# DLRM tower with pairwise field interactions on one Trainium2 core: ScalarE makes one-hot units ahead of its drains, and the last batch chunk has two looked-up field groups instead of four

## The reference

```python
e = jnp.stack([tbl_0[ids[:, 0]], ..., tbl_39[ids[:, 39]]], axis=1)      # 2048 x 40 x 32
i, j = np.triu_indices(40, k=1)
z = jnp.einsum('bke,kef,bkf->bk', e[:, i, :], L0_rec_W, e[:, j, :])      # 2048 x 780
h = jnp.concatenate([z, dense_ctx], axis=1)                              # 2048 x 796
h = jnp.maximum(h @ W_top1 + b_top1, 0.0)                                # 512
h = jnp.maximum(h @ W_top2 + b_top2, 0.0)                                # 256
y = h @ W_top3                                                           # 1
```

## Time and profile before

| | us |
|---|---|
| median of 3 runs | 693.56 |
| the profiled execution's own time | 690.86 |
| its span | 689.1 |
| TensorE busy | 653.5 (95%) |
| VectorE busy | 537.8 (78%) |
| POOL busy | 374.5 (54%) |
| ScalarE busy | 277.2 (40%) |
| TensorE's mean granted clock | 0.993 of full |

### The profile page before, as it was taken

One profiled execution on the slowest core, in us unless ns is written; L12 is line 12 of the kernel. 1 busy time (PEld: TensorE's weight loads), 2 busy tenths in 40 slices (PEclk: granted clock), 3 DMA queues, 4 the chain that ended last, 5 costly groups with the idle time before them and its releaser, 6 DMA issues.

```text
span 689.1 us, 11819 instructions
## 1 busy us (share of the span) xinstructions
PE 653.5 (95%) x5120; PEld 203.5 (30%) x5120; DVE 537.8 (78%) x515; ACT 277.2 (40%) x196; POOL 374.5 (54%) x391
## 2 busy tenths in 40 slices
PE   3779889888999999999999999999999999999998
PEld 1222223222233333233333323333332323223233
DVE  6776789889879898879768989797767878789910
ACT  3634855876636455647034545655210000100002
POOL 5774576666566566565556556565564666560000
PEclk9989999999999999999999999999999999999999
DMA  7392111203320303012311202001202201101000
GB/s 250 103 377 86 48 52 41 58 13 87 79 68 11 87 12 88 10 43 58 87 23 46 87 11 57 10 14 46 66 13 55 55 13 20 48 12 48 1 1 0
DMA packets 26707, 39.40 MB, mean 57 GB/s; under 512 B 9168, under 2 KB 15456, under 8 KB 26528
## 3 DMA queue, kind: packets, MB, share of 16 engines
q1 hardware_dynamic: 14336, 32.33, 14.5%
q0 software_dynamic: 12288, 6.32, 6.1%
q10 hardware_dynamic: 32, 0.01, 0.0%
HBM read 22.88 MB, written 0.01 MB: 33 GB/s over the span
## 4 chain that ended last, share of the span: by engine, by line
PE 89%; ACT 5%; DMA 2%; DVE 2%; SPq 1%; issue 1%; DVEq 0%; ACTq 0%
PE tps L680 31%; PE zps L702 27%; PE mlp_ps L753 15%; PE mlp_ps L733 12%; PE tps L753 4%; ACT hot L534 2%; ACT hot L531 2%; DVE prods L660 2%; DMA eT<-eT 1%; DMA ids<-in_hot_ids 1%; SPq L432 1%; PE zps L689 0%; ACT zs L500 0%; ACT eT L540 0%; PE mlp_ps L758 0%
## 5 line engine op out<-in xcount | busy, mean ns | idle before, releaser
L660 DVE TENSOR_TENSOR prods<-tps,eT 128x1024 f32<-128x1024 f32 x400 | 468.6, 1217 | 109.9 <-PE tps L680 106.4
L484 POOL DMA_INDIRECT rows<-in_table,idx x384 | 373.8, 974 | 245.9 <-DVE prods L660 136.9
L680 PE MATMUL tps<-eT,weights 32*128 32x512 f32 x1600 | 242.9, 643 | 8.3 <-ACT eT L540 6.2
L702 PE MATMUL zps<-prods,select 128*32 128x512 f32 x1600 | 207.4, 607 | 0.8 <-DVE prods L660 0.3
L531 ACT ACTIVATE hot<-ids,minus_code 128x2048 bf16<-128x2048 int16 x57 | 113.7, 1994 | 41.1 <-PE mlp_ps L733 41.0
L733 PE MATMUL mlp_ps<-hot,parts 128*32 128x512 bf16 x1536 | 106.0, 390 | 23.6 <-ACT hot L534 10.8
L534 ACT ACTIVATE hot<-hot,ones 128x2048 bf16<-128x2048 bf16 x57 | 114.1, 2002 | 1.9
L680 PEld LDWEIGHTS tps<-eT,weights 32*128 32x128 f32 x1600 | 70.7, 183 | 135.9 <-DVE prods L660 72.1
L753 PE MATMUL mlp_ps<-zs,w1s 128*128 128x512 f32 x182 | 85.6, 608 | 0.0
L702 PEld LDWEIGHTS zps<-prods,select 128*32 128x32 f32 x1600 | 35.5, 108 | 150.7 <-DVE prods L660 88.5
L500 ACT ACTIVATE zs<-zps 128x512 f32<-128x512 f32 x28 | 16.7, 597 | 150.7 <-PE zps L702 144.5
(11 more groups left out here) (28 smaller groups left out, 44.6 us busy)
## 6 DMA issues: line engine op xcount, KB each, us to landing
ids<-in_hot_ids SPq DMA_DIRECT2D x16, 512.0 KB, 4.9
eT<-eT SPq DMA_DIRECT2D x40, 192.0 KB
rows<-in_table,idx POOLq DMA_INDIRECT x384
eT<-eT SPq DMA_DIRECT2D x40, 128.0 KB
eT<-eT SPq DMA_DIRECT2D x40, 64.0 KB
zs<-in_hot_table SPq DMA_DIRECT2D x4, 512.0 KB, 8.5
w1s<-in_w SPq DMA_DIRECT2D x1, 1792.0 KB
weights<-in_wt SPq DMA_DIRECT2D x1, 960.0 KB, 8.9
```

The source lines that it names most:

```text
L484: pool.indirect_dma_start(rows[:, k % ROW_SLOTS, m * EMB:(m + 1) * EMB], None, table, bass.IndirectOffsetOnAxis(ap=idx[:, g, t, m:m + 1], ...
L660: dve.tensor_tensor(prods[:, at % PROD_SLOTS, 2 * half:2 * half + 2, :], tps[:, (2 * at + half) % PAIR_BANKS, :, :], tiles, ALU.mult).then ...
L680: last = pe.matmul(tps[:, (2 * at + half) % PAIR_BANKS, bank, :], weights[part, n, :], eT[part, slot_of(t, g), :], start=True, stop=True)
L702: last = pe.matmul(zps[EMB * r:EMB * (r + 1), :], select[:, off:off + EMB], prods[:, at % PROD_SLOTS, bank, :], start=kt < KT - 1 and slot ...
```

## The change

It does five things. (1) In the last chunk only groups 0 and 1 are hot; groups 2 and 3 are gathered like the others, so 14 groups are looked up and 26 gathered. (2) The MLP steps done during chunk 2 are cut into twos and threes, as those during chunk 3 are, and units follow only behind as many output tiles as there are hot groups. (3) In chunks 0 and 1 (`HOTS[...][0] < 2`) ScalarE's units of a cycle are made ahead of that cycle's drains. (4) Of groups 2 and 3 of chunk 0 ScalarE makes one unit each, number 5, and not numbers 3 and 7; VectorE makes the others, the fourth unit of group 2 already before its `rest(2, 1)`. (5) VectorE's units of chunk 1's groups are made four quads ahead of use and not three.

```diff
@@ -112,7 +112,7 @@
-HOT_COUNT = (4, 4, 4, 4)
+HOT_COUNT = (4, 4, 4, 2)
@@ -130,7 +130,7 @@
     for at, tile in enumerate(tiles.values()):
-        starts = list(range(0, len(tile) - 1, 2)) if t == CHUNKS - 1 else [0, 4] if at < 2 else [0]
+        starts = list(range(0, len(tile) - 1, 2)) if t > 1 else [0, 4] if at < 2 else [0]
@@ -162,7 +162,7 @@
             blocks.append(batch)
-            if hots and batch[-1][2] == 0 and batch[-1][4] == KT - 1:
+            if batch[-1][2] == 0 and batch[-1][3] < len(hots) and batch[-1][4] == KT - 1:
                 blocks += [(hots[batch[-1][3]], u) for u in range(0, UNITS, 2)]
@@ -189,7 +189,7 @@
     t, g = HOTS[h]
-    return [g > 1 and u % 4 == 3, ((h - HOT_COUNT[0]) * UNITS + u) % 3 > 0, u % 2 == 1][min(t, 2)]
+    return [g > 1 and u == 5, ((h - HOT_COUNT[0]) * UNITS + u) % 3 > 0, u % 2 == 1][min(t, 2)]
@@ -203,14 +203,15 @@
 for unit in range(UNITS):
-    MAKES[1 + unit // HOT_SLOTS].append((3, unit))
+    MAKES[3 if by_scalar(3, unit) else 1 + unit // HOT_SLOTS].append((3, unit))
...
-            MAKES[side_at - (2 if by_scalar(*item[1:]) else 3)].append(item[1:])
+            MAKES[side_at - (2 if by_scalar(*item[1:]) else 4)].append(item[1:])
@@ -561,15 +562,19 @@
             act.wait_ge(consts_built, 2 + Q)
-            make_unit(2, 3)
             round_part(3, 0)
-            make_unit(2, 7)
+            make_unit(2, 5)
             round_part(3, 1)
-            make_unit(3, 3)
             for cycle in CYCLES:
                 at = cycle[0]
                 if at == QUADS + 1:
                     act.wait_ge(mlp_loaded, 16 * 5)
+                units = [unit for quad in cycle for unit in MAKES[quad] if by_scalar(*unit) and unit != (2, 5)]
+                for unit in units:
+                    if HOTS[unit[0]][0] < 2:
+                        make_unit(*unit)
                 drain_tiles(steps_of(at))
                 drain_sums(at - 1)
...
-                for unit in [unit for quad in cycle for unit in MAKES[quad]]:
-                    if by_scalar(*unit) and unit not in ((2, 3), (2, 7), (3, 3)):
+                for unit in units:
+                    if HOTS[unit[0]][0] > 1:
                         make_unit(*unit)
@@ -634,7 +639,7 @@
             rest(2, 0)
-            for u in range(HOT_SLOTS - 1):
+            for u in range(HOT_SLOTS):
                 make_unit(2, u)
```

## The result

In the comparison that the forecast was made for, the changed kernel takes 663.36 us (median of 4 runs, 662.41 to 664.96) and the kernel before 693.29 us (4 runs, 691.1 to 695.09): a ratio of 0.957, 95% interval 0.954 to 0.961, 30 us less. The forecast was 666.1, with 660.5 to 677.

What follows compares the result with a forecast made beforehand. TensorE, busy 95%, was taken as the bound, so time is gained where it stands or gets less work. Terms 5.9 + 10.4 + 1.2 + 10.0 = 27.5 off 690.86 give 663.4, plus 2.7 a 666.1 us median; range 660.5 to 677.

Steps and rivals of the forecast that it cites:

- (a): Chunk 0's start, quads 0 to 6: earlier copies of hot groups 2 and 3 save 5.9 us.
- (b): Chunk 0: all five look-up stalls for ScalarE's units go, 10.4 us; eight quads take 21.7 us.
- (c): Chunk 0: the clock dip behind the stall near 76 us goes with it, saving 1.2 us.
- the loop did not tighten towards TensorE's 20.5: Chunk 0's upper bound: eight quads at 20.5 us, not 21.7, would gain 5 x 1.2 us more.
- VectorE did not close up further: Rival in chunk 0: VectorE's backlog takes half the stall gain and all the clock gain; 672.5 us, chance 0.12.
- (d): Chunk 2: 16 units fewer and finer MLP batches save 10.0 us, with VectorE not taking over.
- (e): 32 more gathers, two transposes, two fewer id loads: no cost, covered by POOL's waits and VectorE's open time.
- The rival that ended on the slow side: Chunk 3: gathers come late because POOL can't go faster, delaying the last transpose by 43.7 us; 737 us, chance 0.03.

Runs made afterwards that it cites:

- e1: Changed kernel with four hot groups in the last chunk and the old MLP batches restored, leaving chunk 0's parts; 808.9 us, 0.987 of the kernel before.
- e4: Kernel before with only chunk 1's ScalarE units made ahead of the cycle's drains; 814.1 us, 0.988 of the kernel before.
- e10: Changed kernel with only the first of each group's 16 gathers issued, the rest left zero; 663.4 us, 0.793 of the kernel before.
- e2: Kernel before with only the last chunk's two hot groups (26 gathered) and chunk 2's fine batches added; 852.3 us, 1.039 of the kernel before.
- e12: Changed kernel with each of the 416 indirect gathers replaced by a plain copy of the same shape; 664.2 us, 0.815 of the kernel before.
- e11: Changed kernel with the gathered ids set to zero, so each gather fetches its tables' first rows; 838.4 us, 1.027 of the kernel before.
- e9: Changed kernel run once more without any edit; 857.4 us, 1.025 of the kernel before.
- e6: Changed kernel with chunk 2's MLP steps back in the old coarse batches; 844.3 us, 1.032 of the kernel before.
- e7: Changed kernel with no hot group in the last chunk, so 28 gathered groups; 928.8 us, 1.135 of the kernel before.

## Why the prediction was right, and where it was not

**Against the first comparison it was right** in its sum and in the stretches, though not in every step inside them. These sizes are read from one trace of the whole change. No part was run alone under those conditions, so that each part causes its own share is argued from where the time left, and supported by the waits in e1 to e4.

*(a) Start.* -5.9 was forecast. From the first product to quad 6 it took 64.68 - 32.54 = 32.1 us and now 59.94 - 33.92 = 26.0: -6.1. The mechanism is the forecast one. ScalarE copies group 2 as soon as its sum is there, and the transform waits 0.70 us, not 4.68:

```profile
42.94 0.60 ACT L541 ACTIVATE eT<-mlp_ps 128x512 f32<-128x512 f32 x1 [7.84 <-PE mlp_ps L738]
...
43.59 0.71 PE L685 MATMUL tps<-eT,weights 32*128 32x512 f32 x4 [0.70 <-ACT eT L541]
```

But the steps inside don't match, and that their sum does is in part luck. The transform was to start at 41.0 and started at 43.59, 9.7 us behind the first product and not 8.5. Group 3's copy was to start at 50.5 and started at 53.40; measured from the first product it came 4.4 us earlier than before, not 5.9. The rest was made up behind it. The forecast let quad 6 wait for the mixed tile as before, while now VectorE works from 55.29 to 61.17 without a pause, and quad 6's products wait for no DMA.

*(b) and (c) Stalls and clock.* -10.4 and -1.2 were forecast. Quad 6 to quad 50 took 195.73 - 64.68 = 131.05 and now 179.98 - 59.94 = 120.04: -11.0. The 40 quads from 10 to 50 take 109.0 us and not 117.1, 21.8 for eight against the 21.7 forecast. So the loop did not tighten towards TensorE's 20.5, and VectorE did not close up further. The cold stretches behind the stalls, at 45.6 and at 76.3 us, are gone; the one at 35 us grew to the full 6.8 us shown above (0.50, where that stretch of before had 0.75), which costs an estimated 1.7 us more at most (0.25 of 6.8 us). The rule of the Trainium skill (TensorE: Matmul & The Clock Gate, Part 1), that activity releases the throttle, fits what went; of the stretch that grew the trace shows only that TensorE had stood 2.8 us ahead of 35.2.

*(d) Chunk 2.* -10.0 was forecast, 158.9 - 148.4 = -10.5 came, with TensorE busy 148.2 of 148.4 and VectorE 125.9, where 125 had been worked out.

*(e) Gathers.* Nothing was forecast, and nothing shows in this trace. The last gather ends 6.8 us ahead of the transpose that needs it (7.9 before), no transpose waits, and POOL's waits for products fell from 136.9 to 72.1 us:

```profile
595.56 0.95 POOL L485 DMA_INDIRECT rows<-in_table,idx  x1 [0.30 <-issue]
```

```profile
603.26 0.70 DVE L617 STREAM_TRANSPOSE eT<-rows 128x512 f32<-128x512 f32 x1
```

The sum of the terms was 27.5 and the stretches lost 27.3. The forecast median is 2.7 us too high. Two errors make that up. I had taken the median to lie 2.7 us above the profiled execution, as before, and it lies 1.6 below it, which makes 4.3. The profiled execution itself took 664.96 and not 663.4, 1.6 the other way, mostly since the first product came 1.4 us later. Both errors are of the size of the spread between runs; that they partly cancel is luck.

**Under the conditions of the later runs it would have been wrong,** and the step is (e). "Nothing, covered by these waits" counts a gather as POOL's time alone. There a gather costs the other engines: 0.50 us each on the mean of e10's 390. The 32 that the change adds cost more than that: e2 lost 32.6 us, 1.0 for each. If chunk 2 kept its forecast saving beneath that, it would be 42.6/32 = 1.3, but no saving shows there: with about as many gathers in it, chunk 2 takes 194 us in e2 and 191 in e1. So term (d), too, which was right in the first comparison, doesn't come out there. The rival that ended on the slow side had the right object and the wrong way: its gathers would be late, with VectorE waiting for `rows`. No trace shows such a wait. The gather beside VectorE's units takes 1.37 us after as it did before, but what was lost is time of TensorE and of those that wait for it. The rule of the Trainium skill (SBUF — State Buffer, Who interferes with whom) is about a two-port operation of VectorE and POOL shutting each other out, and doesn't give that.

Two things stay open. What differs between the first comparison and the later ones isn't known: the same kernel took 693 and 820 us, and the chip of the first comparison isn't on record. And by which way an indirect DMA of POOL holds up TensorE and its signals isn't shown. The traces have the late signals, TensorE's stops where it waits for nothing, the end of both within 2.6 us of the last gather, and the indifference to which rows are read.

**Which version to take.** Under the first conditions the changed kernel is the fastest that was run. Under the later ones it is e1, chunk 0's parts with the old hot groups (0.987 of before; e4, at 0.988, can't be told from it), which wasn't run under the first; by the forecast's terms it would stand near 676 there, an estimate. e12's and e10's times aren't to be had, since they don't fetch the right rows, but they say what a fetch of the same rows in another form could be worth: 174 us (e12 beside e11) to 194 us (e10 beside e9).

## What to carry to other kernels

Put an engine's early work ahead of its waiting work in the queue: a unit whose slot had been free for 10 us stood behind a drain, and the stretch with those stalls became 11 us shorter here once it stood ahead. When busy time decides, price the side work by the chain that ended last, as term (d) did; whether finer batches keep a stretch above the next engine's floor was asked in e6 and stays open. And before trading compute for gathers "that POOL has time for", run the kernel once with most gathers left out and once with plain copies in their place: what they cost elsewhere appears in no row of their own.

## What the runs showed of the hardware

In every later trace with 384 to 448 indirect DMAs issued by POOL, on three chips, TensorE's results reached other engines late, by 27 us at worst in e7 and 9.2 in e9. On the first occasion, with 384 and 416 of them, nothing came more than 0.5 us late. TensorE itself also stopped between matmuls that wait for nothing. Taking 390 of the 416 away took away 194 us (857.4 to 663.4), and 416 plain ones of the same shape in their place gave 664.2 beside 838.4 for indirect ones on the same chip.

Kernels with 24, 26 and 28 gathered groups took 809 to 837, 838 to 857, and 888 to 929 us, though those with more groups give TensorE less to do. In chunk 1, where that work is the same, the cost for each gather rose from 0.41 to 0.58 us as they came closer together. The gathers' own durations are the same either way (969 ns each in the profile after and in e9).
